# List 1 with rows of 536 bytes, logits from the unnormalized rows, and GpSimd's row transfers without their waits for first products

## The reference, cut to what matters

```python
x = x + gat(layernorm(x), adj, W, a)      # x: 64 graphs of 128 nodes, 128 features
x = x + ffn(layernorm(x), gate_w, gate_b, w1, w2, w3)

def gat(h, adj, W, a):                    # per graph
    Wh = h @ W.T
    e = leaky_relu((Wh @ a1)[:, None] + (Wh @ a2)[None, :], 0.2)
    e = where(adj > 0, e, -9e15)
    return softmax(e) @ Wh

def ffn(x, gate_w, gate_b, w1, w2, w3):   # 16 experts, hidden 256, the best 2 of each row
    logits = x @ gate_w + gate_b
    top_probs, top_idx = top_k(softmax(logits), 2)
    top_probs /= sum(top_probs)
    return sum over the two: top_prob * (silu(x @ w1[e]) * (x @ w2[e])) @ w3[e]
```

## Time and profile before

| | us |
|---|---|
| median of 3 runs | 519.61 (518.23 to 519.63) |
| the profiled execution | 513.99 |
| its span, first to last instruction | 512.2 |

### The profile page before, as it was taken

How to read it: one execution, slowest core, us unless ns; L and a number is a source line. 1 busy time by engine, 2 the same in 40 slices (tenths; PEclk the granted TensorE clock), 3 DMA queues, 4 the chain that set the end, 5 groups by cost and what they waited for, 6 DMA issues and landing times.

```text
span 512.2 us, 11503 instructions
## 1 busy us (share of the span) xinstructions
PE 393.6 (77%) x2993; PEld 357.2 (70%) x2994; DVE 250.7 (49%) x978; ACT 224.2 (44%) x583; POOL 257.1 (50%) x284
## 2 busy tenths in 40 slices
PE   6889788867685867079988788852998887888890
PEld 3678677755564766079977788852998887888880
DVE  4788989865786453024433344340342523424250
ACT  2799576563574513024424344320443423525240
POOL 5222346775328666426554655561355554555554
PEclk9999999987887678569999999985899999999996
DMA  3544345646173356577666666424654664555500
GB/s 105 158 130 135 90 154 158 185 155 208 43 228 116 135 178 235 204 236 248 222 221 193 202 215 225 152 71 124 184 182 158 189 186 160 164 179 187 164 28 1
DMA packets 75547, 83.35 MB, mean 163 GB/s; under 512 B 10564, under 2 KB 60111, under 8 KB 75504
## 3 DMA queue, kind: packets, MB, share of 16 engines
q1 hardware_dynamic: 66032, 61.58, 39.7%
q0 software_dynamic: 9472, 21.26, 11.8%
HBM read 36.06 MB, written 28.94 MB: 127 GB/s over the span
## 4 chain that ended last, share of the span: by engine, by line
PE 47%; issue 18%; DVE 10%; SPq 7%; POOL 6%; DMA 4%; ACT 3%; another core or an unknown queue 2%; ACTq 1%; POOLq 0%; DVEq 0%
PE bank L499 26%; PE bank L512 11%; PE bank L371 5%; SPq L303 4%; POOL sorted_rows L1014 3%; POOL rstd L1005 2%; DMA shared<-in_adj_dram 2%; DVE prob L931 1%; DMA R<-sorted_rows 1%; DVE stats L688 1%; SPq L318 1%; DVE h L698 1%; DVE R L744 1%; PE bank L419 1%
## 5 line engine op out<-in xcount | busy, mean ns | idle before, releaser
L499 PE MATMUL bank<-xT,w_t 128*128 128x128 f32 x1280 | 181.9, 285 | 25.2 <-issue 16.4
L499 PEld LDWEIGHTS bank<-xT,w_t 128*128 128x128 f32 x1280 | 164.1, 199 | 30.1 <-issue 19.7
L632 ACT ACTIVATE hT<-bank 128x256 f32<-128x256 f32 x160 | 60.5, 384 | 171.2 <-PE bank L499 97.1
L931 DVE TENSOR_TENSOR prob<-hT,bank 128x256 f32<-128x256 f32 x160 | 67.2, 420 | 136.9 <-ACT hT L632 76.9
L1039 POOL DMA_INDIRECT out_dram<-R x80 | 78.3, 979 | 80.1 <-DVE R L940 51.1
L512 PE MATMUL bank<-W,prob 128*128 x640 | 102.5, 284 | 14.3 <-issue 10.0
L1039 POOL DMA_INDIRECT sorted_rows<-R x80 | 78.4, 980 | 69.5 <-DVE R L940 48.3
L512 PEld LDWEIGHTS bank<-W,prob 128*128 128x128 f32 x640 | 86.8, 196 | 19.5 <-issue 18.6
L940 DVE SCALAR_TENSOR_TENSOR R<-bank,R 128x128 f32<-128x128 f32 x160 | 55.1, 346 | 65.9 <-PE bank L512 56.5
L1014 POOL DMA_INDIRECT sorted_rows<-R,ROW x64 | 62.7, 979 | 29.5 <-issue 16.7
L371 PE MATMUL bank<-ident,R 128*128 128x128 f32 x224 | 39.1, 299 | 45.7 <-DMA R<-sorted_rows 26.5
(11 more groups left out here) (129 smaller groups left out, 382.4 us busy)
## 6 DMA issues: line engine op xcount, KB each, us to landing
R<-sorted_rows SPq DMA_DIRECT2D x160, 130.0 KB
w_t<-W SPq DMA_DIRECT2D x80, 256.0 KB
W<-in_L_ffn_w_dram SPq DMA_DIRECT2D x48, 128.0 KB
sorted_rows<-pad SPq DMA_DIRECT2D x34, 130.0 KB
R<-in_x_dram SPq DMA_DIRECT2D x16, 256.0 KB
shared<-in_adj_dram SPq DMA_DIRECT2D x16, 256.0 KB
sorted_rows<-R POOLq DMA_INDIRECT x80
out_dram<-R POOLq DMA_INDIRECT x80
```

The source lines that it names most:

```text
L499: ins = nc.tensor.matmul(H[k][:, m * P:(m + 1) * P], w_t[:, par, k, m * P:(m + 1) * P], xT[:, par, k * P:(k + 1) * P], start=True, stop=True)
L632: nc.scalar.activation(sil[:, k, :], H[k][:, 0:HC * P], ACT.Silu).then_inc(silu_ready, 1)
L931: V.tensor_tensor(hidT[:, k, :], sil[:, k, :], H[k][:, HC * P:2 * HC * P], ALU.mult).then_inc(hid_ready, 1)
```

## The change

What it does, by place:

- Rows of list 1 have 134 values (536 bytes): x2, the two numbers, two gates, and mean and reciprocal root of the second layernorm. Rows of list 2 keep 260. The 24 blocks of the lists lie in a buffer of their own (`rows`), no longer in `R`.
- The logits are formed from x2: `gw_c` is the gate weight with its column means taken off (one small product at the start, `centre`), and VectorE multiplies the result by the reciprocal root (`logits_scaled`) and adds the bias. The pipeline has 19 iterations; choices, places and the first table come one iteration earlier, and so do the counts in `DISPATCHED` (43 tiles instead of 39 in the loops). ScalarE no longer normalizes for the second layernorm. It normalizes two of the four tiles of each group for the first one, with `shift_of`, which VectorE computes after x2 in the iteration before.
- In TensorE's order the turn of x2 stands first in an iteration, the turn of h before the logits and the attention product.
- VectorE normalizes list 1's rows where the list is processed (`normalize_rows`, two blocks each at the first two places of the quad before). TensorE's `turn_rows` and ScalarE's `copy_rows` of the next quad stand at the third place (`TURN = 2`) instead of the first. Between quads 3 and 4 of list 1 (`early`) nothing overlaps: quad 3's last results are finished before quad 4 is waited for.
- The clears of list 2's tensor stand in SyncE's queue behind the weights of quads 6 and 7, eight at each place.
- GpSimd's waits `PACED` are gone.
- Between the lists TensorE runs 30 matmuls whose result isn't used (`SWITCH`).
- ScalarE's quads 1 to 6 of list 1 are written out as well.

The diff, cut to its core:

```diff
-    LAG, NO = 3, 3
+    LAG, NO, TURN = 3, 3, 2
-    ROW2, DEST, GATE = 2 * D, 2 * D + 1, 2 * D + 2
-    DW = GATE + NL
+    ROW2, DEST, GATE = D, D + 1, D + 2
+    MEAN = GATE + NL
+    RSTD = MEAN + 1
+    WIDTH = (RSTD + 1, D + MEAN)
+    BY_ACT = 2
...
+        R = sb("R", [P, NG, RSTD + 1])
+        rows = sb("rows", [P, RB * QT, D + RSTD + 1])
...
+        def early(c, q, behind):
+
+            return c == 0 and isinstance(q, int) and q == NQA + behind
+        def carried(row, c):
+
+            return row[:, D:D + WIDTH[0]] if c == 0 else row[:, 0:WIDTH[1]]
...
             load_up(3, 1)
-            for b in range(NE // QT):
-                clear_pads(1, b * QT, pad_in[1])
             sp.wait_ge(table_ready, 2)
             sp.wait_ge(dispatched_b, 16 * (NG - GG * FIRST[EARLY]))
...
             for q in (RB, RB + 1):
                 load_quad(0, q, q - RB, 1)
                 load_up(q, q % 2)
+                for b in range(NE // QT // 2):
+                    clear_pads(1, ((q - RB) * (NE // QT // 2) + b) * QT, pad_in[1])
...
+                if c == 0:
+                    pe.wait_ge(h2_ready, q * QT + QT)
+                else:
+                    pe.wait_ge(xs_in[slot], (nth + uses(slot) + 1) * (16 * QT))
...
+                if c:
+                    pe.wait_ge(xT_ready, NQ)
+                    keep_warm(SWITCH, XP)
...
-                        if k == 0 and not last:
+                        if k == TURN and not last and not early(c, q, -1):
                             turn_rows(c, q + 1, (at + 1) % RB, nth + (at + 1) // RB)
...
-                        if k == 0 and not last:
+                        if k == (QT - 1 if early(c, q, -1) else TURN) and not last:
                             copy_rows(c, q + 1, 1 - par)
...
+            def shift_of(i):
+
+                par = i % 2
+                dve.wait_ge(rstd1_ready, i + 1)
+                V.scalar_tensor_tensor(shift[:, par, :], mv[:, par, 0:BY_ACT, 0], -1.0, rstd[:, par, 0:BY_ACT],
+                                       ALU.mult, ALU.mult).then_inc(shift_ready, 1)
...
+            def normalize_rows(q, at, nth, tiles):
+
+                slot = at % RB
+                dve.wait_ge(xs_in[slot], (nth + 1) * (16 * QT))
+                for k in tiles:
+                    r = rows[:, slot * QT + k, :]
+                    V.tensor_scalar(r[:, 0:D], r[:, D:2 * D], r[:, D + MEAN:D + MEAN + 1], r[:, D + RSTD:D + RSTD + 1],
+                                    ALU.subtract, ALU.mult).then_inc(h2_ready, 1)
...
+                        if c == 0 and k < 2 and not last and not early(c, q, -1):
+                            normalize_rows(q + 1, at + 1, nth + (at + 1) // RB, range(2 * k, 2 * k + 2))
...
+            def first_root(i):
+
+                pool.wait_ge(var1_ready, i + 1)
                 if i >= 2:
-                    pool.wait_ge(read, i - 1)
-                g.tensor_tensor(rstd[:, par, col:col + GG], var_eps[:, par, col:col + GG], half_neg[:], ALU.pow).then_inc(rstd_done, 1)
+                    pool.wait_ge(h_by_act, i - 1)
+                    pool.wait_ge(h_by_dve, i - 1)
+                g.tensor_tensor(rstd[:, i % 2, :], var_eps[:, i % 2, 0:GG], half_neg[:], ALU.pow).then_inc(rstd1_ready, 1)
...
-            DISPATCHED = {8: 4, 9: 4, 10: 4, 11: 6, 12: 6, 13: 5, 14: 3, 15: 3, 16: 4}
+            DISPATCHED = {7: 4, 8: 4, 9: 4, 10: 6, 11: 6, 12: 5, 13: 3, 14: 3, 15: 5, 16: 3}
...
-            PACED = {8: 1, 12: 2, 16: 5, 20: 8, 24: 11}
             for m in range(t, NG):
-                if m - t in PACED:
-                    pool.wait_ge(up_done, PACED[m - t])
                 dispatch(m)
```

More of the change, by code:

```diff
@@ L358, in _, with keep_warm @@
             pe.wait_ge(const_steps, 7)
-            for _ in range(WARM):
-                nc.tensor.matmul(RT[:], ones_bf[:], ones_bf[:, 0:1].broadcast_to([P, GG * N]), start=True, stop=True)
+            def keep_warm(n, into):
+                for _ in range(n):
+                    nc.tensor.matmul(into[:], ones_bf[:], ones_bf[:, 0:1].broadcast_to([P, GG * N]), start=True, stop=True)
+            keep_warm(WARM, RT)
             pe.wait_ge(small_in, 80)
-            pe.wait_ge(const_steps, 12)
+            pe.wait_ge(const_steps, 13)
             pe.wait_ge(setup_v, 1)
@@ L374, in iteration @@
             def iteration(i, par, has=lambda k: True, chosen=None):
+                if has(3):
+                    k = i - 3
+                    pe.wait_ge(x2_ready, k + 1)
+                    if later(k, 1):
+                        pe.wait_ge(x2T_ready, k)
+                    turn(TH2, lambda g: R[:, k * GG + g, 0:D], x2_turned)
                 if has(2):
@@ L431, in iteration @@
                 if i == 0:
-                    nc.tensor.matmul(RT[:], ident[:], h2T[:], start=True, stop=True)
+                    nc.tensor.matmul(RT[:], ident[:], x2T[:], start=True, stop=True)
             def choose(b):
@@ L950, in quad @@
                                     table=q if c == 0 and isinstance(q, int) and q in (1, 2) and k == LAG else None)
-                        elif not first:
+                        elif not first and not early(c, q, 0):
                             add_row(c, t + (k - LAG), at + RB - 1, k + (QT - LAG))
```

253 lines of the change are left out of this document (137 added, 116 removed).

## The result

The changed kernel takes 537.54 us (median of 6 runs, 531.01 to 541.59), the kernel before 519.62 (516.46 to 527.76): a ratio of 1.034, 95% interval 1.029 to 1.040. It is 3.4% slower. I had forecast 507.0, range 494 to 519, with 0.14 for slower. The profiled execution took 536.66 us, span 534.9; that of before 512.2.

The account below looks back on a forecast made before the run. TensorE with its own issue bounds the lists; the hole before quad 4 comes from late row requests behind list 1's clears. -18.9 + 10 - 3.5 = -12.4 us from 513.99 gave 501.6, as a median 507.0, range 494 to 519.

Parts of the forecast that it names:

- iterations get 6 us longer: Graph phase: seven iterations with dispatches take about 76.5 us against 70.5 before, bounds 70 and 85.
- The wait for the root: Graph phase: VectorE's shift_of waits for GpSimd's root behind the dispatches; an iteration with n dispatches costs 4.6 + 1.27n us.
- ScalarE's two normalizations: Graph phase: ScalarE takes two of VectorE's four normalizations per iteration; counted at nothing, as neither engine is the constraint.
- the graph phase stretches: Rival, up to quad 4: VectorE's stop for the root adds to instruction stalls, +8 us, 515 in all; chance 0.10.
- Quad 3 starts 22.3 us behind PADS.: List 1: PADS at 175.6, then SyncE's clears and the weight load; quad 3 starts at 197.9 instead of 202.93.
- 209.3: List 1: forecast start of quad 4, against 228.18 before: -18.9 us, bounds -11 and -26.
- SyncE asks for quad 4 at about 196.: SyncE's queue: without list 1's clears quad 4's rows are requested at about 196, landed at 199.8, under quad 3's cover.
- 80 normalizations, hidden, bound +3: List 1 on VectorE: 80 normalizations of 0.34 us, 27 us, beside 47.8 busy of 122: hidden, bound +3.
- The clears: List 1, quads 6 to 8: moved clears delay rows of quads 7 and 8, +10 us, bounds 3 and 17.
- The switch: Between the lists: thirty matmuls let list 2's first 8 us run at the upper clock, -3.5 us, bounds -4 and +1.4.
- The late turn: Rival, both lists: turning at the third product makes ScalarE's copy late, 1 us in some 38 quads, +38, 545; chance 0.13.
- The rule against the change: List 1: VectorE's normalizations may lock GpSimd's sends out, about 3 us by the rule; by the trace row none.

Follow-up runs that it names:

- second series: The follow-up runs, later, on four chips: the kernel before takes 446.2 to 446.8 us by the medians, the changed kernel 471.7.
- the old order: Changed kernel with TensorE's logits, attention product, count and turn of h back in their order before the change: 466.5 us against 471.7.
- the shift last: Changed kernel with VectorE's shift_of, which waits for GpSimd's root, moved to the end of the iteration: 461.2 us against 471.7.
- first series: The runs of the result, chip not on record: kernel before 519.62 us, changed kernel 537.54.

## Why the prediction was wrong

**The step that failed first is "iterations get 6 us longer".** The wait for the root was named and its place was right; the size was not. Seven iterations took 84.8 us, the upper bound of my range (70 to 85), not 76.5; in the second series 81.0 against 62.8. They also began later, at 67.2 and not at the 61.8 that I took over from the kernel before: the iterations ahead of the first dispatch had become longer too, for which the sum had no term. My sum for an iteration (two roots, dispatches, VectorE's tail) had none either for what else goes round the loop: TensorE's attention product, behind a turn of h that waits for ScalarE's two normalizations, and the count for which TensorE stands while VectorE chooses. Taking the root wait away gave 10.4 us, the old order 5.2; that these two waits are the whole of it is not shown, since with the shift last the seven iterations still take 74.2 us. The rival "the graph phase stretches" was the right one, at 0.10 and with +8; it was +13 at PADS. I also counted ScalarE's two normalizations at nothing because ScalarE is not the constraint; that it is the order in which TensorE waits for them that counts fits the old order's gain, but no edit took them off ScalarE.

**"Quad 3 starts 22.3 us behind PADS."** I had the landing of its weights set this, as before. The weights were sent as forecast, 22.0 us behind PADS, and quad 3 started 12.7 us later, at 34.6, because quads 0 to 2 were not done: the normalizations of each next quad stand on VectorE behind the last placing, the tables and the gated products, and ScalarE had its stop of 9.1 us. In the second series it is 23.8 us, with the weights sent by 12.1; there the turn of quad 1 waits 4.7 us for normalizations. In the kernel before the turn of quad 1 was done ahead of PADS. Quad 4 then came 14.4 us behind quad 3 instead of 11.4. With the late PADS (194.57, not 175.6) this is the whole of the 34.3 us by which quad 4 missed its 209.3.

**"SyncE asks for quad 4 at about 196."** It asked at 223.35. The dispatches started last at 208.85 and not near 192, the sixteen clears for list 0 took 19.5 us and not 16.5, and the table of block numbers, written in quad 1, was not in my list of what must be there: in the kernel before it was 22 us ahead of the request, in the changed one 0.5 us. This miss cost nothing here, since quad 3 was later still; with quads 0 to 3 on time it could be next. My two rates for SyncE also compared different transfers: 1.03 us was a clear beside a busy GpSimd, 0.50 a load of rows, while the clears at 201.12, with GpSimd busy for 6.87 of 18 us, took 0.96 each. Removing what is last asks for the whole list of what the instruction waits for, each with its new time.

**"80 normalizations, hidden, bound +3".** Share of busy time was the wrong measure. In the second series this was the dearest part, 14.7 us by the edit that moved them by one step. In the first series it was 79.9 us from quad 7's first product to quad 18's in both kernels, 7.3 us a quad, so there the normalizations were hidden in the later quads. How much of the first series' 17.9 us is theirs stays open, since no edit ran there.

**The clears** had +10 in the sum. The mechanism is there: in the kernel before TensorE stands 3.3 and 4.3 us for late rows with them, and their new place costs 11.1. In the changed kernel, for which the sum was made, it costs 3.1 by the medians of the second series (6.8 by the stages), and in the first VectorE stood 0.5 us for rows in list 1: the eight clears took 5.2 and 4.9 us there, and the quads were slower than the 5.8 us that I had. So +10 was too much, and 11.1 does not bear it out. What they block was mis-sized too: 8.3 us in the kernel before, not most of 15, for the dispatches were right behind them, and nothing that shows in the changed one (32.6 us from PADS to quad 4 in the second series, 32.8 before).

**The switch**, -3.5: not seen. List 2's first 8 us ran at a mean of 0.61 after all, and the experiments put it at zero.

**The late turn**, my only rival with the right sign, gave nothing in the second series, so its 0.14 was not spent on the mechanism that did it there. In the first series one of its signs is there: the 12.4 us that TensorE stood for copies in list 2, which was 4.5 us longer than before. How much of these 4.5 is the turn's stays open. Had I added the bounds in one direction (+15 for the graph phase, nothing gained at quad 4) I would have seen a slower case that needs no late copy.

**The rule against the change** (the Trainium skill, "SBUF — State Buffer", "Who interferes with whom") had its test here: list 1's sends, beside 80 normalizations, took a mean of 984 ns, list 2's, beside none, 981. By these rows the sends do not lengthen, as the prediction had taken it.

```profile
L1120 POOL DMA_INDIRECT sorted_rows<-rows x80 | 78.7, 984 | 78.1 <-DVE rows L1012 48.4 <-issue 29.7
L1120 POOL DMA_INDIRECT out_dram<-rows x80 | 78.5, 981 | 84.3 <-DVE rows L1012 66.0 <-issue 18.3
L936 DVE TENSOR_SCALAR rows<-rows 128x128 f32<-128x128 f32 x80 | 24.6, 360 | 0.6 <-DMA rows<-sorted_rows 0.5
```

## What to carry to other kernels

Work added to an engine with time to spare is hidden only if it stands on the right side of that engine's wait: look for where the engine is idle in a period and put the work ahead of the instruction that ends the idle time, not behind it. A wait on a short reciprocal root is cheap by its own row and dear in a loop, since statistics, eps, root and dispatches all stand behind it; move the instruction that waits to where nothing is queued behind it. When the last of several things that an instruction waits for is removed, write down all the others with their new times; and transfers with no reader for 100 us belong behind the loads, not between them.

## What the runs showed that I had not expected

The same kernel before takes 519.6 us in one series and 446.7 in the other, with single operations of equal length (GpSimd's sends 980 ns in either); ratios moved too, 1.034 in one and 1.054 in the other, so a part's price in us does not carry over where it is hidden in gaps between instructions. Whether the chip makes the difference is not shown. And edits did not add: an order that gains 5.2 us alone loses 8.7 beside another edit that itself gains 10.4.
